# Up-projection of a fused cross-attention block: each group of 512 tokens accumulated in two halves of 256

## The chip, the cores and the metric

The kernel runs on one core of a Trainium2 chip. The metric is the device time of one execution in microseconds (us); lower is better. A measured time is the median of several executions.

## The reference

One transformer block with cross-attention, for a batch of 8, with 1024 query tokens and 64 context tokens per batch, width 512, 16 heads and a feed-forward width of 2048, all in float32:

```python
q = layer_norm(query, ln1_g, ln1_b)
qh, kh, vh = q @ wq + bq, context @ wk + bk, context @ wv + bv      # 16 heads of 32
probs = softmax(where(allowed, qh @ kh.T / sqrt(32), -inf))
x = query + (probs @ vh) @ wo + bo
h = layer_norm(x, ln2_g, ln2_b)
out = x + gelu(h @ w1 + b1) @ w2 + b2
```

The part that the change touches is `h @ w1`, the up-projection: 8192 tokens, 512 inputs, 2048 outputs.

## The kernel before

**Numbers.** A float32 product is made of three float16 products: every operand is scaled and split into a high and a low half, and `triple` accumulates high by high, high by low and low by high in PSUM, for each of the four blocks of 128 inputs. So a product over 512 inputs is 12 matmuls into one accumulation, each with a weight load of its own.

**Tiling.** The 8192 tokens are 16 chunks of 512 (`CHUNK`; `HALF` is 256). The program runs 17 slots. In slot c the attention of chunk c and the feed-forward of chunk c-1 are interleaved, so that the small dependent steps of attention are covered by feed-forward matmuls. In slot 0 there is no feed-forward, in slot 16 no attention.

**A slot on TensorE.** The loop over g has `GROUPS` = 19 turns. A turn with g below 16 makes the up-projection group g: 128 of the 2048 hidden features (the stationary operand is a 128x128 cut of `w1`) for all 512 tokens of the chunk (the moving operand is `old`, the normalised tokens with features on partitions, in the arena), into the PSUM bank `ff1_ps[:, g % 2, :]`, 128 x 512 float32. The last of the group's matmuls counts `ff1_done` up. A turn with g of 3 or more (`LAG`) makes the down-projection of group g-3 at L1384: 12 matmuls of 512 columns, whose four outputs stay in `ff2_ps` over all 16 groups. Between the two stand the attention steps that the table `PLAN` gives for that place: "Q" (48 matmuls, L1141), "S" (the scores, L1298: 24 matmuls of 128 columns; they use 64 of the 128 rows each, alternately the lower and the upper half), "V" (L1318) and "O" (L1141). All instructions of TensorE stand in one order written by the program; a slot has 624 matmuls when it has both parts.

**Who waits for a group.** ScalarE waits for `ff1_done`, reads the whole bank at L753 (gelu), then VectorE makes the two float16 halves of the result (L1114, L829). The next group but one may write the bank when the gelu is out (`g_full`); the down-projection waits for the halves (`g_lo`). In the trace `ff_ps` is both `ff1_ps` and `ff2_ps`, `at_ps` the two banks of attention, `w_all` the weights `w1` or `w2`, `act_T` and `arena` activations.

**Line L1141.** All calls of `triple` have this one line in the profile; rows are told apart by their tiles: `ff_ps<-arena,w_all` is the up-projection (3072 matmuls: 16 slots by 16 groups by 12), `at_ps<-act_T,wq` is Q and `at_ps<-wo,act_T` is O.

Of the kernel before, what the change touches and what calls it, by code (L numbers as in the profile page):

```python
# [18 lines left out]
KT = D // P  # L19
# [9 lines left out]
CHUNK = 512  # L29
TT = CHUNK // P  # L30
HALF = CHUNK // 2
# [70 lines left out]
def wait(eng, sem, value):  # L102

    if isinstance(value, int) and value <= 0:
        return
    eng.wait_ge(sem, value)


def cross_attention_block(nc, x, context, wq, wk, wv, bq, bk, bv, wo, bo,
# [5 lines left out]
    with ExitStack() as ctx:  # L115
# [144 lines left out]
        ff1_ps = ctx.enter_context(nc.psum_tensor("ff1_ps", [P, 2, CHUNK], F32))  # L260
# [109 lines left out]
        def plan(c, position):  # L370

            if isinstance(c, int) and c == 0:
                return PLAN_FIRST.get(position, [])
            second = PLAN_SECOND.get(position, []) if isinstance(c, int) and c == 1 else []
            return PLAN.get(position, []) + second
# [758 lines left out]
        def _(pe):  # L1134
            def triple(out_ap, pairs):

                last, n = None, 3 * len(pairs)
                i = 0
                for (s_hi, s_lo), (m_hi, m_lo) in pairs:
                    for s, m in ((s_hi, m_hi), (s_hi, m_lo), (s_lo, m_hi)):  # L1140
                        last = nc.tensor.matmul(out_ap, s, m, start=(i == 0), stop=(i == n - 1))  # L1141
                        i += 1
                return last
# [4 lines left out]
            for k in range(KT):  # L1148
                for n in range(KT):
                    last = nc.tensor.transpose(ff2_ps[:, k, n * P:(n + 1) * P], ctx_raw[:, n, k * P:(k + 1) * P],  # L1150
                                               ident[:, :])
# [5 lines left out]
            def maximum_rows(n):  # L1157

                if n < len(ROUNDS) - 1:
                    pe.wait_ge(max_ready[n], 1)  # L1160
                wait(pe, sums_ready, (0, 1, 3, N1 + 3, N1 + N2 + 3)[n])
                nc.tensor.transpose(turned[n], maxima[:, ROUNDS[n]], ident[:, :]).then_inc(rows_ps[n], 1)

            def maxima_everywhere(n):
                pe.wait_ge(diagonal_set[n], 1)
                nc.tensor.matmul(spread[n], ones[0:widths[n], :], on_diagonal[0:widths[n], n, 0:widths[n]],
                                 start=True, stop=True).then_inc(gmax_ps[n], 1)

            def bias_rows(n, ln_b, weight):


                quarter = P // KT
                for k in range(KT):
                    for m in range(KT):
                        w = weight(k, m)
                        last = nc.tensor.matmul(bias_bank[n][m * quarter:(m + 1) * quarter, 0:w.shape[-1]],
                                                cols[:, ln_b + k:ln_b + k + 1].to_broadcast([P, quarter]), w,
                                                start=(k == 0), stop=(k == KT - 1))
                last.then_inc(bias_rows_ps[n], 1)

            def bias_columns(n, width, rows):

                pe.wait_ge(bias_rows_set[n], 1)
                for b in range(width // P):
                    last = nc.tensor.transpose(bias_cols[n][:, b * P:(b + 1) * P], rows[:, b * P:(b + 1) * P],
                                               ident[:, :])
                last.then_inc(biases_ps[n], 1)
# [29 lines left out]
            def keys(k, m):  # L1217
                cut = slice(m * P, (m + 1) * P)
                return term(ff1_ps[:, m % 2, :], k, (wk_hi[:, k, cut], wk_lo[:, k, cut]), (ctxT_hi[:, k], ctxT_lo[:, k]))


            for k in range(KT):
                pe.wait_ge(ctx_lo, k + 1)
                pe.wait_ge(conv_lo, k + 1)
                for m in range(2):
                    last = keys(k, m)
# [5 lines left out]
            for m in range(2, KT):  # L1232
                pe.wait_ge(kv_hi, m - 1)
                for k in range(KT):
                    last = keys(k, m)
# [21 lines left out]
            def slot(c, par, attn, ff, batch):  # L1257
# [82 lines left out]
                old = hT[1 - par]  # L1340
                for g in range(GROUPS):
                    if isinstance(c, int) and c == 0 and 2 * g == BIAS_ROWS_AT:
                        for n in range(N1):
                            pe.wait_ge(w_loaded[W_1 + n], 16)
                        bias_rows(1, B2LN, lambda k, m: w1_raw[m][:, k])
                    if isinstance(c, int) and c == 0 and 2 * g == BIAS_COLUMNS_AT:
                        bias_columns(1, D, bias_rows_sb)
                    if ff and g < NJ:
                        if g % KT == 0 and isinstance(c, int) and c == 1:
                            pe.wait_ge(conv_lo, conv_w1[g // KT])  # L1350
                        if g == 0 and isinstance(c, int) and c == 1:
                            pe.wait_ge(h_lo, 4)
                        elif g == 0:
                            for n in range(TT):
                                pe.wait_ge(h_moved[n], 16 * c + (-16))
                        if g >= 2:
                            pe.wait_ge(g_full, NJ * c + (g - 1 - NJ))
                        else:
                            wait(pe, g_full, NJ * c + (-NJ))
                        cut = slice(g % KT * P, (g % KT + 1) * P)  # L1360
                        w1_hi, w1_lo = (w1_pairs[:, g // KT, a] for a in range(2))
                        triple(ff1_ps[:, g % 2, :], [((w1_hi[:, k, cut], w1_lo[:, k, cut]), (old[:, 0, k], old[:, 1, k]))
                                                     for k in range(KT)]).then_inc(ff1_done, 1)
                    if attn:
                        for kind, t in plan(c, 2 * g):
                            step(kind, t)
                    if isinstance(c, int) and c == 0:
                        for n, (rows_at, spread_at) in REDUCE_AT.items():
                            if 2 * g == rows_at:
                                maximum_rows(n)  # L1370
                            if 2 * g == spread_at:
                                maxima_everywhere(n)
                    if ff and g >= LAG:
                        j = g - LAG
                        pe.wait_ge(g_lo, NJ * c + (j + 1 - NJ))
                        if j == 0:
                            wait(pe, out_set, 4 * c + (-TT))
                        if isinstance(c, int) and c == 1:
                            pe.wait_ge(conv_lo, conv_w2[j // KT] - KT + j % KT + 1)
                        pair = g_pair[j % NG]  # L1380
                        for t in range(TT):
                            rows = slice(t * P, (t + 1) * P)
                            for i, (s, m) in enumerate(((0, w2_hi), (0, w2_lo), (1, w2_hi))):
                                last = nc.tensor.matmul(ff2_ps[:, t, :], pair[:, s, rows], m[:, j],  # L1384
                                                        start=(j == 0 and i == 0), stop=(j == NJ - 1 and i == 2))
                            if j == NJ - 1:
                                last.then_inc(ff2_done, 1)
                    if attn:
                        for kind, t in plan(c, 2 * g + 1):
                            step(kind, t)  # L1390


            for c in range(NCHUNK):
                slot(c, c % 2, True, c > 0, None if c % 2 else c // 2)
            slot(NCHUNK, 0, False, True, None)


# [18 lines left out]
```

## Time and profile before

| | us |
|---|---|
| median of 3 runs | 1868.79 |
| lowest and highest run | 1867.86, 1869.2 |
| span of the profiled execution (first to last instruction) | 1864.5 |
| TensorE busy in it | 1799.3 |
| VectorE, ScalarE, GpSimd busy in it | 1247.9, 640.5, 443.8 |

The profiled execution gives a span and no time of its own apart from it. The runs' median is 4.3 us above the span; that rest is the start and the end of the program around its instructions.

In the rows, PE is TensorE's matmuls, PEld its weight loads (which run beside matmuls), DVE is VectorE, ACT ScalarE, POOL GpSimd. Matmuls are pipelined: a matmul's recorded duration goes beyond the start of the next one, so the rate of a stream is read from starts, not from durations.

### The profile page before, as it was taken

The page shows a single profiled execution, that of the slowest core. Times are in us where ns is not written, and L with a number is a line of the kernel's source. Part 1 is how long each engine was busy: PE and PEld are TensorE (multiplying, and loading weights), DVE is VectorE, ACT ScalarE, POOL GpSimd, SP SyncE. Part 2 cuts the span into 40 slices and gives each one's busy share as a digit, 9 for nine tenths or more (in the row PEclk, how much of TensorE's full clock was granted, in tenths as well). Part 3 has the DMA queues.
Part 4 walks back from the last instruction along what each step waited for, and adds up shares of the span by engine and source line. Part 5 has one row for each costly group of instructions (what it writes and reads, how often), then busy time and mean ns, then how long its engine had stood idle before and what let it go on. Part 6 is the DMA issues. An engine that isn't in the chain of part 4 may idle for free.

```text
span 1864.5 us, 26584 instructions
## 1 busy us (share of the span) xinstructions
PE 1799.3 (97%) x10213; PEld 819.6 (44%) x10213; DVE 1247.9 (67%) x1930; ACT 640.5 (34%) x799; POOL 443.8 (24%) x376
## 2 busy tenths in 40 slices
PE   6678899999999999999999999999999999999999
PEld 3233344444444444444444444444444444444444
DVE  6767757667675767757676676757677576866622
ACT  5654424242232424223242422324242232424211
POOL 2523114131320314122141313203141221413200
PEclk8878999999999999999999999999999999999999
DMA  8230232314123241412323131332413133231200
GB/s 288 54 105 12 46 91 46 91 23 79 35 60 77 46 91 23 78 36 57 80 46 91 19 81 38 57 80 46 91 21 77 40 57 79 46 91 19 50 23 23
DMA packets 287738, 116.27 MB, mean 62 GB/s; under 512 B 262616, under 2 KB 264192, under 8 KB 287616
## 3 DMA queue, kind: packets, MB, share of 16 engines
q1 hardware_dynamic: 287616, 114.61, 27.4%
q8 instruction: 80, 1.31, 0.3%
q14 instruction: 42, 0.34, 0.1%
HBM read 31.22 MB, written 16.78 MB: 26 GB/s over the span
## 4 chain that ended last, share of the span: by engine, by line
PE 90%; DVE 5%; POOL 1%; ACT 1%; DMA 1%; issue 1%; SPq 0%; DVEq 0%; ACTq 0%
PE ff_ps L1141 34%; PE ff_ps L1384 34%; PE at_ps L1141 18%; PE at_ps L1298 2%; PE at_ps L1318 1%; DVE w_all L829 1%; POOL arena L560 1%; DVE arena L829 0%; DVE xhat L818 0%; DMA arena<-in_L_xattn_wk 0%; PE ff_ps L1213 0%; DVE arena L1114 0%; DVE arena L1061 0%; PE at_ps L1213 0%; DVE smax L1059 0%
## 5 line engine op out<-in xcount | busy, mean ns | idle before, releaser
L1141 PE MATMUL ff_ps<-arena,w_all 128*128 128x512 f16 x3072 | 701.8, 381 | 2.3 <-DVE arena L829 2.3
L1384 PE MATMUL ff_ps<-w_all,arena 128*128 128x512 f16 x3072 | 698.0, 379 | 0.9 <-DVE arena L829 0.9
L1141 PEld LDWEIGHTS ff_ps<-arena,w_all 128*128 128x128 f16 x3072 | 300.4, 98 | 371.7 <-issue 15.6
L1384 PEld LDWEIGHTS ff_ps<-w_all,arena 128*128 128x128 f16 x3072 | 294.4, 98 | 358.6 <-issue 6.4
L753 ACT ACTIVATE arena<-ff_ps,b1p,scales 128x512 f32<-128x512 f32 x256 | 198.5, 775 | 634.6 <-PE ff_ps L1141 634.3
L1114 DVE TENSOR_SCALAR arena<-arena,scales 128x512 f16<-128x512 f32 x256 | 150.1, 586 | 215.6 <-ACT arena L753 215.5
L829 DVE SCALAR_TENSOR_TENSOR arena<-arena,scales 128x512 f16<-128x512 f32 x256 | 239.2, 934 | 9.1
L511 POOL TENSOR_TENSOR rstd<-ve,minus_half 128x1 f32<-128x1 f32 x128 | 85.6, 669 | 561.1 <-DVE ve L801 561.1
L555 POOL TENSOR_TENSOR x_sb<-x_sb,bo_row 128x512 f32<-128x512 f32 x64 | 92.6, 1477 | 359.8 <-PE at_ps L1298 350.5
L687 ACT ACTIVATE norm_hl<-xhat 128x512 f16<-128x512 f32 x120 | 73.9, 628 | 287.6 <-DVE xhat L818 287.6
L560 POOL TENSOR_TENSOR arena<-arena,rsum 128x1024 f32<-128x1024 f32 x64 | 124.8, 1971 | 176.1 <-DVE rsum L1087 176.1
L1141 PE MATMUL at_ps<-act_T,wq_hi 128*128 128x512 f16 x496 | 150.0, 384 | 9.9 <-DMA act_T<-norm_hl 9.9
L1141 PE MATMUL at_ps<-wo_hi,act_T 128*128 128x512 f16 x512 | 156.9, 383 | 2.1 <-DVE act_T L829 2.1
L1044 DVE CAST qT<-arena 128x512 f16<-128x512 f32 x64 | 31.3, 489 | 125.8 <-ACT arena L691 125.8
L691 ACT ACTIVATE arena<-at_ps,bqp,scales 128x512 f32<-128x512 f32 x64 | 49.7, 778 | 159.5 <-PE at_ps L1141 155.9
L1141 PE MATMUL at_ps<-wo_lo,act_T 128*128 128x512 f16 x256 | 98.1, 383 | 0.0
L1141 PE MATMUL at_ps<-act_T,wq_lo 128*128 128x512 f16 x248 | 95.1, 384 | 0.0
L829 DVE SCALAR_TENSOR_TENSOR act_T<-at_ps,act_T 128x512 f16<-128x512 f32 x68 | 43.9, 685 | 65.3 <-ACT act_T L714 65.3
L566 POOL TENSOR_TENSOR arena<-arena,b_row 128x512 f32<-128x512 f32 x64 | 87.3, 1394 | 0.9 <-DVE xhat L818 0.9
L825 DVE TENSOR_TENSOR norm_hl<-xhat,norm_hl 128x512 f16<-128x512 f32 x120 | 83.2, 693 | 5.1 <-ACT norm_hl L687 3.6
L1059 DVE TENSOR_REDUCE smax<-at_ps 128x16 f32<-128x1024 f32 x54 | 64.9, 1202 | 26.9 <-PE at_ps L1298 26.9
L1099 DVE SCALAR_TENSOR_TENSOR arena<-at_ps,scales,x_sb 128x512 f32<-128x512 f32 x64 | 48.0, 749 | 49.6 <-PE at_ps L1141 44.4
(154 smaller groups left out, 1377.3 us busy)
## 6 DMA issues: line engine op xcount, KB each, us to landing
x_sb<-in_x SPq DMA_DIRECT2D x64, 256.0 KB, 2.8
out_x<-arena SPq DMA_DIRECT2D x64, 256.0 KB, 2.1
w_all<-in_L_xattn_w SPq DMA_DIRECT2D x6, 1024.0 KB, 11.6
arena<-in_L_xattn_w SPq DMA_DIRECT2D x2, 1024.0 KB, 15.8
v_sb<-v_sb SPq DMA_DIRECT2D x6, 192.0 KB, 3.0
arena<-in_ctx SPq DMA_DIRECT2D x1, 1024.0 KB, 5.2
arena<-in_L_xattn_wk SPq DMA_DIRECT2D x1, 1024.0 KB, 7.4
arena<-in_L_xattn_wq SPq DMA_DIRECT2D x1, 1024.0 KB, 7.4
```

The lines of the kernel that those rows point to most:

```text
L511: nc.gpsimd.tensor_tensor(rstd[:, n:n + 1], ve[:, n:n + 1], minus_half[:, :], ALU.pow).then_inc(ln_rstd, 1)
L555: nc.gpsimd.tensor_tensor(x_sb[:, t], x_sb[:, t], bo_row[:, :], ALU.add).then_inc(xb_set, 1)
L560: nc.gpsimd.tensor_tensor(pr, pr, rsum[:, t, :].unsqueeze(2).to_broadcast([P, HEADS, SC]), ALU.mult).then_inc(p_norm, 1)
L566: nc.gpsimd.tensor_tensor(x1[1 - par][:, t], x1[1 - par][:, t], b2_row[:, :], ALU.add).then_inc(x1b_set, 1)
L687: nc.scalar.activation(norm_hl[:, t, 0], xhat[:, t % 2], ACT.Copy).then_inc(n_hi, 1)
L753: nc.scalar.activation(gelu_full[g % 2], ff1_ps[:, g % 2, :], ACT.Gelu, bias=b1p[:, g:g + 1], scale=col(C1)).then_inc(g_full, 1)
L825: nc.vector.tensor_tensor(norm_hl[:, t, 1], xhat[:, t % 2], norm_hl[:, t, 0], ALU.subtract).then_inc(n_lo, 1)
L829: nc.vector.scalar_tensor_tensor(lo, src, factor, hi, ALU.mult, ALU.subtract).then_inc(done, 1)
L1059: nc.vector.tensor_reduce(smax[:, t, :], scores, AX_X, ALU.max).then_inc(s_max, 1)
L1114: nc.vector.tensor_scalar(pair[:, 0, :], gelu_full[g % 2], col(SG), None, ALU.mult).then_inc(g_hi, 1)
L1141: last = nc.tensor.matmul(out_ap, s, m, start=(i == 0), stop=(i == n - 1))
L1384: last = nc.tensor.matmul(ff2_ps[:, t, :], pair[:, s, rows], m[:, j], start=(j == 0 and i == 0), stop=(j == NJ - 1 and i == 2))
```

## The change

The 12 matmuls of an up-projection group, each of 512 tokens, become two runs of 12 matmuls of 256 tokens: the first accumulates tokens 0 to 255 into the left half of the bank, the second tokens 256 to 511 into the right half. Both use the same 12 stationary operands in the same order, and each matmul loads its own again. `ff1_done` is counted up once, by the last matmul of the second half. Nothing else is changed.

```diff
-                        triple(ff1_ps[:, g % 2, :], [((w1_hi[:, k, cut], w1_lo[:, k, cut]), (old[:, 0, k], old[:, 1, k]))
-                                                     for k in range(KT)]).then_inc(ff1_done, 1)
+                        for part in (slice(0, HALF), slice(HALF, CHUNK)):
+                            last = triple(ff1_ps[:, g % 2, part], [((w1_hi[:, k, cut], w1_lo[:, k, cut]),
+                                                                    (old[:, 0, k, part], old[:, 1, k, part]))
+                                                                   for k in range(KT)])
+                        last.then_inc(ff1_done, 1)
```

The order of instructions on TensorE in an ordinary slot, around one scores step, before (`128x512` is the shape of the moving operand; `waits` are the semaphores for which the first instruction of a row waits):

```order
L1384 MATMUL ff_ps<-w_all,arena 128x512 x11
L1141 MATMUL ff_ps<-arena,w_all 128x512 [waits g_full]
L1141 MATMUL ff_ps<-arena,w_all 128x512 x11
L1298 MATMUL at_ps<-arena,qT 128x128 [waits s_sub]
L1298 MATMUL at_ps<-arena,qT 128x128 x23
L1384 MATMUL ff_ps<-w_all,arena 128x512 [waits g_lo]
```

The same place after the change (three lines more in the file make L1384 into L1387):

```order
L1387 MATMUL ff_ps<-w_all,arena 128x512 x11
L1141 MATMUL ff_ps<-arena,w_all 128x256 [waits g_full]
L1141 MATMUL ff_ps<-arena,w_all 128x256 x23
L1298 MATMUL at_ps<-arena,qT 128x128 [waits s_sub]
L1298 MATMUL at_ps<-arena,qT 128x128 x23
L1387 MATMUL ff_ps<-w_all,arena 128x512 [waits g_lo]
```

The group has 24 matmuls of 256 columns in place of 12 of 512, and still one wait, at its first. No instruction has changed its place among the others, and the orders of the other four engines are the same.

Around the step "V" of the same slot, before:

```order
L1384 MATMUL ff_ps<-w_all,arena 128x512 x12
L1318 MATMUL at_ps<-arena 32x512 x24
L1141 MATMUL ff_ps<-arena,w_all 128x512 x12
L1318 MATMUL at_ps<-arena 32x512 x24
L1384 MATMUL ff_ps<-w_all,arena 128x512 x12
```

And after:

```order
L1387 MATMUL ff_ps<-w_all,arena 128x512 x12
L1318 MATMUL at_ps<-arena 32x512 x24
L1141 MATMUL ff_ps<-arena,w_all 128x256 x24
L1318 MATMUL at_ps<-arena 32x512 x24
L1387 MATMUL ff_ps<-w_all,arena 128x512 x12
```

Here too only the group itself differs.

## Rows read from the trace of the kernel before

**Rows 1.** The page: busy times, granted clock by slice, chain that ended last.

```profile
span 1864.5 us, 26584 instructions
...
PE 1799.3 (97%) x10213; PEld 819.6 (44%) x10213; DVE 1247.9 (67%) x1930; ACT 640.5 (34%) x799; POOL 443.8 (24%) x376
...
PEclk8878999999999999999999999999999999999999
...
PE ff_ps L1141 34%; PE ff_ps L1384 34%; PE at_ps L1141 18%; PE at_ps L1298 2%; PE at_ps L1318 1%; DVE w_all L829 1%; POOL arena L560 1%; DVE arena L829 0%; DVE xhat L818 0%; DMA arena<-in_L_xattn_wk 0%; PE ff_ps L1213 0%; DVE arena L1114 0%; DVE arena L1061 0%; PE at_ps L1213 0%; DVE smax L1059 0%
```

**Rows 2.** Busy time in stretches, PE alone: length, busy (matmuls), clock, DMA.

```profile
1000.00:1108.88 108.88, 108.88 (x626) 1.00 0.28 59
...
360.00:1700.00 1340.00, 1340.00 (x7664) 1.00 0.27 58
```

**Rows 3.** Waits of PE, 120 to 1864 us: total, times, longest.

```profile
PE at_ps L1141 <- DMA act_T<-norm_hl: 9.9, 1, 9.9
PE at_ps L1318 <- DMA arena<-qT: 5.5, 1, 5.5
PE ff_ps L1141 <- DVE arena L829: 2.3, 1, 2.3
```

**Rows 4.** The page's costliest groups: the gelu and what it waits for.

```profile
L753 ACT ACTIVATE arena<-ff_ps,b1p,scales 128x512 f32<-128x512 f32 x256 | 198.5, 775 | 634.6 <-PE ff_ps L1141 634.3
```

**Rows 5.** The chain that ended last, in order of time: start, length, matmuls.

```profile
1005.64 10.36 PE ff_ps L1384 x48
1016.00 10.36 PE ff_ps L1141 x48
```

**Rows 6.** Timeline of PE from 1060 us: start, length with the last one's tail.

```profile
1059.71 0.38 PE L1141 MATMUL ff_ps<-arena,w_all 128*128 128x512 f16 x1
1060.02 0.84 PE L1298 MATMUL at_ps<-arena,qT 64*128 64x128 f16 x24
1060.80 2.76 PE L1384 MATMUL ff_ps<-w_all,arena 128*128 128x512 f16 x12
1063.40 2.75 PE L1141 MATMUL ff_ps<-arena,w_all 128*128 128x512 f16 x12
1065.99 2.75 PE L1384 MATMUL ff_ps<-w_all,arena 128*128 128x512 f16 x12
```

**Rows 7.** Timeline of PE, first slot: two scores steps back to back.

```profile
57.01 0.84 PE L1298 MATMUL at_ps<-arena,qT 64*128 64x128 f16 x24 [2.06 <-DVE qT L1046]
57.69 1.26 PE L1298 MATMUL ff_ps<-arena,qT 64*128 64x128 f16 x24
```

**Rows 8.** Timeline of PE, first slot: part of O, below full clock.

```profile
102.15 1.06 PE L1141 MATMUL at_ps<-wo_hi,act_T 128*128 128x512 f16 x2
103.00 0.63 PE L1141 MATMUL at_ps<-wo_lo,act_T 128*128 128x512 f16 x1
103.43 1.06 PE L1141 MATMUL at_ps<-wo_hi,act_T 128*128 128x512 f16 x2
```

**Rows 9.** Short stretches of PE: length, busy (matmuls), granted clock, DMA.

```profile
101.00:105.00 4.00, 4.00 (x11) 0.50 0.54 114
...
211.00:215.00 4.00, 4.00 (x11) 0.51 0.00 0
```

**Rows 10.** Durations of single instructions at L1141 and L1298: ns min/median/max.

```profile
L1141 PEld LDWEIGHTS ff_ps<-arena,w_all x3072: 95/98/152, 120.9 to 1850.1; 128*128 128x128 f16 x192
...
L1298 PEld LDWEIGHTS at_ps<-arena,qT x1488: 92/94/148, 57.0 to 1713.9; 64*128 64x128 f16 x186
L1298 PE MATMUL at_ps<-arena,qT x1488: 215/216/312, 57.0 to 1714.0; 64*128 64x128 f16 x186
```

**Rows 11.** Timeline of PEld, the weight loads of a group in rows 6.

```profile
1063.18 2.47 PEld L1141 LDWEIGHTS ff_ps<-arena,w_all 128*128 128x128 f16 x12
```

**Rows 12.** The page: the queue that brings instructions (packets, MB, share).

```profile
q8 instruction: 80, 1.31, 0.3%
```

**Rows 13.** Timeline of PE in slot 1, behind its second wait.

```profile
210.75 4.82 PE L1141 MATMUL ff_ps<-arena,w_all 128*128 128x512 f16 x12
```

## The prediction

> **What bounds the kernel now.** I read the page first: TensorE's matmuls fill 97% of the span, no other engine passes 67%, and the chain that ended last runs through matmul lines almost alone, the up-projection with 34% of it [rows 1]. The stretches say it more sharply: between 360 and 1700 us TensorE is busy in all of the 1340 us at a granted clock of 1.00, which is the 2.4 GHz level, and one slot takes 108.88 us with not a gap in it [rows 2]. The longest waits of TensorE after 120 us are of 9.9, 5.5 and 2.3 us [rows 3], and since that stretch has no idle time, they lie before it (the program's order puts them into slot 1). The reader of the changed bank, ScalarE's gelu, spends 634 us idle waiting for the up-projection [rows 4]. So from slot 2 on a time added to a matmul stream is added to the span one for one, and everything else gains slack; the question is only what the stream of 256-column matmuls costs against that of 512.
>
> **The rate of the stream now.** In the chain, 48 matmuls of 512 columns take 10.36 us, in the down-projection and in the up-projection alike [rows 5]: 10.36 / 48 = 215.8 ns each. A change of group costs nothing on top: 1063.40 to 1065.99 is 2.59 us for 12, again 215.8 [rows 6], though the next group has another bank and other operands. At 2.4 GHz, with a column per cycle (the half-clock rows below bear that out), 512 columns last 512 / 2.4 = 213.3 ns. So 2.5 ns of each matmul are not columns, if the clock in this stretch is the full one.
>
> **Is the 2.5 ns paid by the matmul or by the column?** This decides the case: twice as many matmuls carry the same columns. Two kinds of rows answer.
> First the scores step, the shortest matmuls here (128 columns, 53.3 ns at 2.4 GHz). Its 24 go alternately to the two halves of the rows; its 24 in rows 7 take 57.69 - 57.01 = 0.68 us, far less than 24 times 53.3 ns, so two run side by side, and a pair takes 0.68 / 12 = 56.7 ns, 3.4 ns over its columns [rows 7]. The block begins with a load that nothing hides; after such a start the next group's first matmul takes about 0.01 us more (2.76 against 2.75 [rows 6]), and without it the pair is at 55.8 ns, 2.5 over its columns. Reading steps of 0.01 us are worth 0.8 ns here, so the cost at 128 columns is 1.7 to 3.4 ns.
> Second, at half clock: three matmuls of O take 103.43 - 102.15 = 1.28 us [rows 8] where the granted clock is 0.50, the 1.2 GHz level [rows 9]. That is 426.7 ns each, exactly 512 / 1.2, and 1.977 times 215.8, not twice. A cost in proportion to columns would double with the clock; this one is there at full clock and gone at half.
> So the extra is a fixed 2.5 ns per matmul at full clock, and a matmul of 256 columns takes 106.7 + 2.5 = 109.2 ns.
>
> **Are the doubled weight loads hidden?** There are 3072 more. A load of 128 columns is recorded at 98 ns [rows 10]. The loads of the group that starts at 1063.40 begin at 1063.18 [rows 11], one matmul ahead: each load lies under the matmul before its own. At 109.2 ns there is room for 98, with 11 to spare; and the scores show that less room is enough, since loads recorded at 94 ns are followed by matmuls every 56.7 ns on the same half of the rows [rows 7, 10]. I cost them at nothing. Where that cover fails, it can be read too: the scores' rows differ from the group's before them, the load comes only behind it, and the first scores matmul starts 0.31 us after the last of the group (1059.71 to 1060.02 [rows 6]) and not 0.216: 0.09 us for one uncovered load.
> The Trainium skill, page "TensorE: Matmul & The Clock Gate", section "Back-to-back issue gap", speaks against the change: with a weight load per matmul it gives a sustained 81 ns at 128 columns, well over the columns' time. Section "LDWEIGHTS (loading the stationary operand)" of the same page gives a load as columns divided by 1.2, an estimate of 107 ns here, which would leave 2 ns of room. This trace has 56.7 ns where the page has 81, and 98 where it has 107; by the page's 25 ns over, paid by each new matmul, the estimate would be some 140 us more, by the rows nothing.
>
> **The other parts.** (a) Instructions: the queue that brings them moved 1.31 MB in 80 packets [rows 12] for 20,426 matmuls and loads [rows 1], about 64 bytes each; 6,144 more are 0.39 MB or 24 packets. It is at 0.3% of the DMA engines, and TensorE has taken 24 loads and 24 matmuls in 0.68 us [rows 7] where a changed group has 2.6 us for as many. Nothing. (b) The count of `ff1_done` and the wait for `g_full` stay one per group, at its end and its start. The gelu cannot start on the first half, so there is no gain from it; it starts as much later as the group has become longer, and its engine waits anyway [rows 4]. (c) The bank: before, 12 matmuls added to the same 512 columns one after the other; now to the same 256. The scores do the same on 128 at the fixed cost above. Nothing.
>
> **The sum.** A group has 12 matmuls more: 12 x 2.5 = 30 ns. Of 256 groups, 9 do not count. Four stand in slot 1 before its 9.9 us wait and four between the last scores step and the 5.5 us wait [rows 3], both for transposes that do not depend on them. One, at 210.75, runs at the half-clock level [rows 9, 13], where there is no fixed cost. So 247 x 12 = 2964 added matmuls x 2.5 ns = 7.4 us. The span becomes 1864.5 + 7.4 = 1871.9; the runs' median stands 4.3 us above the span (1868.79 - 1864.5), which I leave as it is: **1876.2 us**, 0.4% slower.
> Its bounds: 2.5 ns is sure at 512 columns; at 128 it is 1.7 to 3.4. At 256, a third of the way from 128 to 512, that leaves 2.0 to 3.1. A pair of halves then costs twice that less 2.5, 1.4 to 3.7 ns more than the whole, and 2964 times that is 4.3 to 11.0 us: 1873.1 to 1879.8.
>
> **Rivals.**
> A. The cost goes by the column (the clock is really a little under 2.4 GHz where 1.00 is shown), and two halves are as long as the whole. Then nothing changes: 1868.8 us, not slower. For it: a clock of 1.00 has two digits, and 2.5 ns is 1.2%. Against it: a scores pair would take 128 x 215.8 / 512 = 54.0 ns, 0.65 us for rows 7's 0.68; and the half-clock rows show no such part. It decides below 1.9 ns per matmul at 256 columns (2 x 1.9 - 2.5 = 1.3 ns, 3.7 us in all, 0.2% of the time, which is about what a measurement here tells from no change). 7%.
> B. Loads show. In its small form, at the seam, the first load of the second half is not taken ahead and costs 0.09 us in 247 groups, 22 us: 1898 us. In its large form each short matmul pays for its load what a scores pair pays over its columns when the uncovered start is spread on it: 1060.80 - 1060.02 = 0.78 us for 12 pairs is 65 ns, 11.7 over 53.3 [rows 6], so 2 x 118.4 - 215.8 = 21 ns for 2964, 62 us: 1938 us. For it: the room of 11 ns is thin beside 98. Against it: no group change shows a seam, and full rows should not need more than two half-row loads in 56.7 ns. It decides where load and hand-over together pass 109 ns. The page's 81 ns is a rule of this kind. 5%.
>
> **How the numbers follow.** The forecast has 87%, A 7%, B 5%; 1% is left for a gain that I have no mechanism for. Faster by over 0.2%: 1%. Within 0.2%: A and the lowest edge of the forecast, 8%. Slower: 91%. The range is the forecast's own, 1873 to 1880 us; A and B together may stay outside.
>
> **What would show it.** In the profile after: 6144 up-projection matmuls of 256 columns, 96 of them in 10.48 us where 48 took 10.36; a group 2.62 us in place of 2.59; a slot 109.36 in place of 108.88; loads still at 98 ns, one matmul ahead; no new wait of TensorE between 360 and 1700 us; the down-projection still at 2.59. If 96 take 10.36, A holds; if the first matmul of the second half comes 0.2 us after the one before it, B's seam; if all stand 118 ns apart, B's large form. I would be wrong in another way if the longer program itself let TensorE wait for its instructions, as gaps without a releaser.

## The result and the profile after

The changed kernel takes 1875.77 us (median of 4 runs, 1874.94 to 1877.4); the kernel before, beside it, 1868.73. The ratio is 1.0041, with a 95% interval of 1.0027 to 1.0056: about 7.0 us slower. The forecast was 1876.2 us, and slower.

From the page of the changed kernel, the lines that answer to [rows 1], [rows 4] and [rows 12], and the costliest matmul and load groups:

```profile
span 1873.1 us, 32728 instructions
...
PE 1806.7 (96%) x13285; PEld 1121.4 (60%) x13285; DVE 1247.9 (67%) x1930; ACT 640.6 (34%) x799; POOL 444.1 (24%) x376
...
PEclk8878999999999999999999999999999999999999
...
q8 instruction: 104, 1.70, 0.4%
...
L1141 PE MATMUL ff_ps<-arena,w_all 128*128 128x256 f16 x6144 | 709.5, 274 | 2.3 <-DVE arena L829 2.3
L1387 PE MATMUL ff_ps<-w_all,arena 128*128 128x512 f16 x3072 | 698.0, 379 | 1.6 <-DVE arena L829 1.6
L1141 PEld LDWEIGHTS ff_ps<-arena,w_all 128*128 128x128 f16 x6144 | 602.2, 98 | 121.7 <-issue 9.3
L753 ACT ACTIVATE arena<-ff_ps,b1p,scales 128x512 f32<-128x512 f32 x256 | 198.6, 776 | 640.0 <-PE ff_ps L1141 639.6
```

TensorE has 3072 matmuls and 3072 loads more. The loads are recorded at the same 98 ns. VectorE, ScalarE and GpSimd are as busy as before to 0.3 us; ScalarE's idle time behind the up-projection has grown from 634.3 to 639.6 us, so it takes the longer groups as slack. The instruction queue moved 0.39 MB in 24 packets more, as forecast.

The rate itself, from the chain of the changed kernel that ended last (start, length, matmuls), which answers to [rows 5]:

```profile
1775.98 10.36 PE ff_ps L1387 x48
1786.34 10.48 PE ff_ps L1141 x96
```

10.48 / 96 = 109.2 ns for a matmul of 256 columns, against 10.36 / 48 = 215.8 for one of 512, in the same execution. Two halves take 218.3, 2.5 ns more than the whole. The timeline of the changed kernel's TensorE (start, length with the last one's tail) shows where in a group it lies:

```profile
1002.42 2.78 PE L1141 MATMUL ff_ps<-arena,w_all 128*128 128x256 f16 x24
1005.04 2.75 PE L1387 MATMUL ff_ps<-w_all,arena 128*128 128x512 f16 x12
1007.63 2.78 PE L1141 MATMUL ff_ps<-arena,w_all 128*128 128x256 f16 x24
```

A group begins 2.62 us before what follows it, where [rows 6] had 2.59; the down-projection is still at 2.59. From one step V to the same step of the next slot the traces have 108.89 us before and 109.37 after. A stretch of the changed kernel, cut at the forecast 109.36 us, shows TensorE busy in all of it (length, busy, clock, DMA; above it the long stretch), to be held against [rows 2]:

```profile
360.00:1700.00 1340.00, 1340.00 (x9969) 1.00 0.28 59
1000.00:1109.36 109.36, 109.36 (x817) 1.00 0.27 59
```

No wait was added in it. The waits of the changed kernel's TensorE after 120 us (total, times, longest) are those of [rows 3]; the last has grown by 0.7 us:

```profile
PE at_ps L1141 <- DMA act_T<-norm_hl: 9.8, 1, 9.8
PE at_ps L1318 <- DMA arena<-qT: 5.4, 1, 5.4
PE ff_ps L1141 <- DVE arena L829: 2.3, 1, 2.3
PE ff_ps L1387 <- DVE arena L829: 1.6, 1, 1.6
```

The two profiled spans differ by 8.6 us, more than the medians. The end of the last wait shows why. First the kernel before, then the changed one, from the timelines of their TensorE:

```profile
251.03 2.76 PE L1384 MATMUL ff_ps<-w_all,arena 128*128 128x512 f16 x12 [0.92 <-DVE arena L829]
```

```profile
252.44 2.76 PE L1387 MATMUL ff_ps<-w_all,arena 128*128 128x512 f16 x12 [1.61 <-DVE arena L829]
```

From here to the end it is 1864.5 - 251.03 = 1613.47 us before and 1873.1 - 252.44 = 1620.66 after: 7.19 us more, for the 240 groups of slots 2 to 16, 30 ns each. The other 1.4 us lie ahead of it, in the start and in slot 1, where this point also moves between kernels whose groups are alike (252.44 to 254.01 us in the runs below with 24 matmuls a group). The tables below therefore give the time from this point to the end too, as "tail". It scatters far less: the change, inter and uneven, whose groups are as long as each other, have tails within 0.1 us.

### The profile page after: what moved, and what is told of

Same layout as the page of the kernel before. It is cut to its first block, busy times and chain, and to the rows that moved or that the text cites. A ratio compares the mean times of both kernels' runs of the same rounds, so it can differ in the third digit from the quotient of the medians.

```text
span 1873.1 us, 32728 instructions
## 1 busy us (share of the span) xinstructions
PE 1806.7 (96%) x13285; PEld 1121.4 (60%) x13285; DVE 1247.9 (67%) x1930; ACT 640.6 (34%) x799; POOL 444.1 (24%) x376
## 4 chain that ended last, share of the span: by engine, by line
PE 90%; DVE 5%; POOL 1%; ACT 1%; DMA 1%; issue 1%; SPq 0%; DVEq 0%; ACTq 0%
PE ff_ps L1141 34%; PE ff_ps L1387 34%; PE at_ps L1141 17%; PE at_ps L1298 2%; PE at_ps L1318 1%; DVE w_all L829 1%; POOL arena L560 1%; DVE arena L829 0%; DVE xhat L818 0%; DMA arena<-in_L_xattn_wk 0%; PE ff_ps L1213 0%; DVE arena L1114 0%; DVE arena L1061 0%; PE at_ps L1213 0%; DVE smax L1059 0%
## 5 line engine op out<-in xcount | busy, mean ns | idle before, releaser
L1141 PE MATMUL ff_ps<-arena,w_all 128*128 128x256 f16 x6144 | 709.5, 274 | 2.3 <-DVE arena L829 2.3
L1387 PE MATMUL ff_ps<-w_all,arena 128*128 128x512 f16 x3072 | 698.0, 379 | 1.6 <-DVE arena L829 1.6
L1141 PEld LDWEIGHTS ff_ps<-arena,w_all 128*128 128x128 f16 x6144 | 602.2, 98 | 121.7 <-issue 9.3
L1387 PEld LDWEIGHTS ff_ps<-w_all,arena 128*128 128x128 f16 x3072 | 294.4, 98 | 330.9 <-issue 6.4
L753 ACT ACTIVATE arena<-ff_ps,b1p,scales 128x512 f32<-128x512 f32 x256 | 198.6, 776 | 640.0 <-PE ff_ps L1141 639.6
L1141 PE MATMUL at_ps<-act_T,wq_hi 128*128 128x512 f16 x496 | 150.1, 385 | 9.8 <-DMA act_T<-norm_hl 9.8
L1141 PE MATMUL at_ps<-wo_hi,act_T 128*128 128x512 f16 x512 | 157.0, 383 | 2.1 <-DVE act_T L829 2.1
L1141 PE MATMUL at_ps<-wo_lo,act_T 128*128 128x512 f16 x256 | 98.1, 383 | 0.0
L1141 PE MATMUL at_ps<-act_T,wq_lo 128*128 128x512 f16 x248 | 95.2, 384 | 0.0
L1141 PEld LDWEIGHTS at_ps<-act_T,wq_hi 128*128 128x128 f16 x496 | 48.9, 99 | 69.8 <-issue 12.9
L1141 PEld LDWEIGHTS at_ps<-wo_hi,act_T 128*128 128x128 f16 x512 | 50.5, 99 | 64.9 <-issue 5.7
```

The lines of the kernel that those rows point to most:

```text
L753: nc.scalar.activation(gelu_full[g % 2], ff1_ps[:, g % 2, :], ACT.Gelu, bias=b1p[:, g:g + 1], scale=col(C1)).then_inc(g_full, 1)
```

## The experiments

The theory: at full clock each matmul has a fixed 2.5 ns that its columns do not explain, and the doubled loads are hidden. The rivals: the cost comes with the weight loads; it comes at the start of the second accumulation or at the change between halves; loads would show soon. Every edit is to the up-projection group unless said otherwise. "Tail more" is against the 1613.47 us of the kernel before, and each time stands beside the kernel before on the same chip.

| run | us | before, us | ratio, 95% interval | tail more, us |
|---|---|---|---|---|
| change | 1875.77 | 1868.73 | 1.0041, 1.0027 to 1.0056 | 7.19 |
| quarters | 1892.09 | 1867.32 | 1.0133, 1.0118 to 1.0149 | 21.61 |
| extra_loads | 1868.24 | 1867.32 | 1.0004, 0.9995 to 1.0013 | 0.59 |
| inter | 1875.42 | 1867.32 | 1.0042, 1.0029 to 1.0056 | 7.28 |
| uneven | 1876.35 | 1867.32 | 1.0044, 1.0030 to 1.0058 | 7.22 |
| both | 1882.31 | 1868.11 | 1.0080, 1.0065 to 1.0096 | 14.40 |
| eighths | 1919.23 | 1868.11 | 1.0276, 1.0261 to 1.0292 | 50.80 |
| uneven32 | 1901.25 | 1868.11 | 1.0180, 1.0166 to 1.0194 | 33.02 |
| halves_extra_loads | 1876.79 | 1867.45 | 1.0048, 1.0034 to 1.0062 | 7.99 |
| uneven_extra_loads | 1950.67 | 1867.45 | 1.0445, 1.0429 to 1.0461 | none: no wait at this point |

**quarters: four accumulations of 128 tokens.**

```diff
-                        for part in (slice(0, HALF), slice(HALF, CHUNK)):
+                        for part in (slice(n * P, (n + 1) * P) for n in range(KT)):
```

> Each group as four accumulations of 128 tokens, 48 matmuls in place of 12. Fixed cost per matmul (2.5 ns at full clock, loads hidden): 36 x 2.5 = 90 ns for each of 247 groups, 22.2 us over the kernel before, 1890.9 us; a matmul every 55.8 ns, the group 2.68 us. Cost by the column: 1868.7. Loads that must have ended (98 ns as recorded) before their matmul starts: a matmul every 98 ns at least, 2.1 us per group, some 2390 us. The page's sustained 81 ns would be 1.3 us per group, some 2190 us (an estimate).

Measured 24.8 us over the kernel before, its interval 22.0 to 27.8; the tail has 21.61, and 240 groups at 90 ns are 21.6. The chain of this run:

```profile
1790.19 10.36 PE ff_ps L1387 x48
1800.56 10.72 PE ff_ps L1141 x192
```

10.72 / 192 = 55.8 ns: 53.3 of columns and 2.5. It is the same fixed part at 128 columns, now on all 128 rows and with a full load for each; no spacing of 98 ns shows. Nor does the sustained 81 ns that the Trainium skill gives for 128 columns (page "TensorE: Matmul & The Clock Gate", section "Back-to-back issue gap"): the measurement decides, 55.8 ns.

**extra_loads: the kernel before, each load made twice.** As many loads as in the change, as many matmuls as before.

```diff
+                                nc.tensor.ldweights(s[:, k, cut])
                                 last = nc.tensor.matmul(ff1_ps[:, g % 2, :], s[:, k, cut], old[:, m, k],
```

> The kernel before, with 12 matmuls of 512 tokens per group, and every weight load of the up-projection made twice: as many loads as in the halved kernel, as many matmuls as before. Fixed cost per matmul: two loads (2 x 98 ns) hide under one matmul (215.8), 1868.7 us. Cost that comes with each load: 2.5 ns x 2964 more loads, 1876.1 us. If only one load can stand ready and the second waits until the first is used up: up to 98 ns for each of 3072, 2170 us.

The page of this run shows that the loads were made, its chain that they cost nothing in the stream:

```profile
PE 1801.4 (97%) x10213; PEld 941.3 (50%) x13285; DVE 1248.4 (67%) x1930; ACT 640.6 (34%) x799; POOL 443.9 (24%) x376
```

```profile
1769.92 10.36 PE ff_ps L1388 x48
1780.28 10.36 PE ff_ps L1365 x48
```

10.36 for 48, as before. The interval holds no change and excludes 7 us. So the 2.5 ns does not come with a load; it comes with a matmul. One thing stays untested: every matmul of every run has a load of its own, so a price for taking over the loaded operand, paid once per matmul, cannot be told from a price of the matmul itself.

The 0.59 us in the tail can be placed. They lie behind the step V that stands before an up-projection group, where no matmul hides the group's first loads. First the kernel before, then this run, from the timelines of their TensorE:

```profile
1084.21 0.84 PE L1318 MATMUL at_ps<-arena 64*32 64x512 f16 x24
1084.98 2.76 PE L1141 MATMUL ff_ps<-arena,w_all 128*128 128x512 f16 x12
```

```profile
1086.00 0.84 PE L1318 MATMUL at_ps<-arena 64*32 64x512 f16 x24
1086.82 2.77 PE L1365 MATMUL ff_ps<-arena,w_all 128*128 128x512 f16 x12
```

From V's start to the group's it is 0.77 us before and, read in ns, 0.81 here: 0.039 us more in each of 14 slots, 0.55 us. So an extra load that no matmul covers does cost, some 40 ns.

**inter: both halves in turn for each stationary operand, one accumulation start for the bank.**

```diff
+                        for k in range(KT):
+                            for i, (s, m) in enumerate(((w1_hi, 0), (w1_hi, 1), (w1_lo, 0))):
+                                for part in (slice(0, HALF), slice(HALF, CHUNK)):
+                                    last = nc.tensor.matmul(ff1_ps[:, g % 2, part], s[:, k, cut], old[:, m, k, part],
+                                                            start=(k == 0 and i == 0 and part.start == 0),
...
```

> The same 24 matmuls of 256 tokens per group as in the change, in another order: for each of the 12 stationary operands both halves in turn, as one accumulation over the bank, so that the second half never starts an accumulation of its own and each stationary operand is loaded twice in a row. Fixed cost per matmul: as the change, 1875.8 to 1876.2 us. A cost of 30 ns at the start of the second accumulation: 1868.7. A cost for changing between halves: 23 changes per group in place of 1, far above 1876.

This run is as long as the change, in time and in tail, and its up-projection too takes 10.48 us for 96. So neither a second accumulation nor the changes between halves cost anything that shows; the number of matmuls counts.

**uneven: 448 and 64 tokens.**

```diff
-                        for part in (slice(0, HALF), slice(HALF, CHUNK)):
+                        for part in (slice(0, 7 * SC), slice(7 * SC, CHUNK)):
```

> Halves of unequal size, 448 and 64 tokens: 24 matmuls per group and the same columns. Fixed cost per matmul with loads hidden even under 64 columns (26.7 + 2.5 = 29.2 ns): as the change, 1876 us. If a load of all rows needs 56 ns of its own (what a pair of half-row loads is seen to fit into in the scores): 27 ns for 12 x 247 matmuls, 80 us, 1956. If it needs the 98 ns recorded: 69 ns each, 204 us, 2080. A granted clock that falls in the groups would add to any of these.

The time is that of the change again. TensorE's timeline of this run (a row is named by its first matmul's shape):

```profile
1009.20 2.78 PE L1141 MATMUL ff_ps<-arena,w_all 128*128 128x448 f16 x24
1011.82 3.40 PE L1387 MATMUL ff_ps<-w_all,arena 128*128 128x512 f16 x15
```

The group takes 1011.82 - 1009.20 = 2.62 us, as in the change, though half of its matmuls offer a load only some 29 ns of cover.

**both: the down-projection in halves too.** Each of its matmuls becomes two of 256 columns, in turn, as in inter.

```diff
-                                last = nc.tensor.matmul(ff2_ps[:, t, :], pair[:, s, rows], m[:, j],
+                                for part in (slice(0, HALF), slice(HALF, CHUNK)):
+                                    last = nc.tensor.matmul(ff2_ps[:, t, part], pair[:, s, rows], m[:, j, part],
...
```

> The change, and the down-projection's matmuls too in halves of 256 columns (each stationary operand used for both halves in turn). Fixed cost per matmul: 3072 more matmuls in a second place, of which 240 to 250 groups count, 7.2 to 7.5 us over the change, 14.6 over the kernel before, 1882 us. A cost that belongs to the up-projection or its bank alone: 1876. The next group's first load starts up to 0.1 us later, which should hide.

The tail grows by 14.40 us, which is 480 groups at 30 ns. The chain of this run:

```profile
1783.19 10.48 PE ff_ps L1388 x96
1793.67 10.48 PE ff_ps L1141 x96
```

The price is the same in another loop, with other operands and another bank, and adds up.

**eighths: eight accumulations of 64 tokens**, by the same edit with parts of 64.

> Each group as eight accumulations of 64 tokens, 96 matmuls, a whole group at 29.2 ns each. Fixed cost per matmul: 84 x 2.5 = 210 ns for 247 groups, 51.9 us over the kernel before, 1919 us, the group 2.80 us. If the loads hide only in short bursts of such matmuls (12 in the run with 448 and 64) and not in 96: more, up to 98 ns each, 9.4 us per group. If the granted clock falls to its lower level in them, the group takes up to twice as long and the 512-column matmuls behind it too.

```profile
1817.82 10.36 PE ff_ps L1387 x48
1828.18 11.20 PE ff_ps L1141 x384
```

In its chain 11.20 / 384 = 29.2 ns, 26.7 and 2.5; 240 x 210 ns is 50.4 of the 50.80 us in the tail. The granted clock stays at 1.00 between 360 and 1700 us, without a gap.

**uneven32: 480 and 32 tokens**, by the edit of uneven with 32.

> Unequal halves of 480 and 32 tokens: 24 matmuls per group, the same columns. Fixed cost per matmul with hidden loads (32 columns: 13.3 + 2.5 = 15.8 ns): 1876 us, as the change. If a full load and its hand-over need up to the 29.2 ns that the 64-column matmuls of the run with 448 and 64 took (the shortest seen so far): up to 13.4 ns for each of 2964, 40 us more, 1916.

Here the fixed price ends. The chain of this run:

```profile
1800.72 10.37 PE ff_ps L1387 x48
1811.09 10.91 PE ff_ps L1141 x96
```

A pair takes 10.91 / 48 = 227.3 ns; with 202.5 for 480 columns (200.0 and 2.5, and so the starts in the trace stand), 24.8 are left for 32 columns, where 13.3 + 2.5 would be 15.8. Both numbers of the expectation missed; 9.0 ns for 2880 matmuls are 25.9 us of its tail.

**halves_extra_loads and uneven_extra_loads: each load twice, in the change and in uneven**, by the edit of extra_loads.

> The change, with every weight load of the up-projection made twice: two loads to each matmul of 256 columns (109.2 ns). If a load takes 98 ns of the array's time as recorded, two do not fit: 196 in place of 109.2, 87 ns for each of 6144 matmuls, some 530 us more than the change. If a load takes no more than the 29.2 ns that a load and a 64-column matmul were seen to need, two hide with room to spare: 1876 us, as the change.

> Halves of 448 and 64 tokens, with every weight load made twice: two loads to each matmul of 29.2 ns. If the 24.8 ns at which the 32-column matmuls stood is the time of a load, two take 49.6 ns, 20.4 more for 12 matmuls of 247 groups, 60 us: 1936. If the 24.8 ns is a floor of the matmul itself and a load takes less than 14.6 ns, nothing changes: 1876. In the run of 512 columns with doubled loads the second load was recorded 41 ns after the first; if that is the time of a load, two take 82 ns, 53 more for each of 2964, 157 us: 2033.

Two loads hide under one matmul of 256 columns: the chain has 10.48 us for 96 (last line of the first fence), and the time is that of the change. Its tail has 0.80 us more than the change, 0.55 us of it again behind the step V. Under 64 columns two loads show. The second fence is TensorE's timeline of uneven_extra_loads, the third its matmuls of 64 columns from the third to the twelfth (the last of its first row stands again as its second row):

```profile
1777.83 10.36 PE ff_ps L1389 x48
1788.19 10.48 PE ff_ps L1366 x96
```

```profile
1007.25 3.10 PE L1366 MATMUL ff_ps<-arena,w_all 128*128 128x448 f16 x24
1010.18 2.75 PE L1389 MATMUL ff_ps<-w_all,arena 128*128 128x512 f16 x12
```

```profile
1009.62 0.72 PE L1366 MATMUL ff_ps<-arena,w_all 128*128 128x64 f16 x10
1010.14 0.20 PE L1366 MATMUL ff_ps<-arena,w_all 128*128 128x64 f16 x1
```

That group takes 2.93 us in place of 2.62, 26 ns more for each of the 12 short matmuls on average. Inside, they stand (1010.14 - 1009.62) / 9 = 58 ns apart, where with one load they stood 29.2. All three values of the expectation missed, the nearest being 49.6. So a load in such a stream takes some 29 ns or less, not the 98 recorded. Whether the 24.8 ns of uneven32 is a load or a floor of the matmul stays open: one load fits into 24.8 ns there, but two take 58 and not 49.6 here.

**Not tried:** a gelu that starts when the first half is done. Both halves lie in one PSUM bank, and nothing in the program would then order ScalarE's reading of it against TensorE's writing of the second half.

## Why the prediction was right

**What bounds it.** That a time added to the stream is added to the span held from slot 2 on: 240 groups at 30 ns, and 7.19 us in the tail.

**2.5 ns per matmul, not per column.** This was the step that decided. Chains give it at 512 and 256 columns (215.8 and 109.2), at 128 (55.8) and at 64 (29.2), on all rows; extra_loads takes the load out of the question, inter the seam. The scores block from which the prediction read its 128 columns was indeed at full clock, which the prediction did not show (length, busy, clock of the kernel before):

```profile
57.01:57.69 0.68, 0.68 (x25) 1.00 0.00 0
```

In ns, the pairs of that block stand 56 apart but for the first step, which is 66 to 67: the 0.01 us that the prediction took off for the start was right. The half-clock step has its counterpart in slot 1 of the changed kernel, in the group that answers to [rows 13]. The first line is the stretch (length, busy, clock), the other two are TensorE's timeline; the last matmul of the row of 16 is the first of the row behind it:

```profile
211.60:215.40 3.80, 3.80 (x19) 0.50 0.00 0
```

```profile
211.80 3.62 PE L1141 MATMUL ff_ps<-arena,w_all 128*128 128x256 f16 x16
215.00 0.63 PE L1141 MATMUL ff_ps<-arena,w_all 128*128 128x256 f16 x2
```

(215.00 - 211.80) / 15 = 213.3 ns for a matmul of 256 columns at the lower level, 256 / 1.2 exactly and half of the 426.7 of [rows 8]: no price there. (The clock rises within this group, in both kernels: its last matmuls stand 110 ns apart here. So the group as a whole is no test.) What the 2.5 ns is made of no run shows.

**Loads at nothing.** Right, with far more room than the 11 ns that were read off the record: extra_loads and halves_extra_loads hide twice as many where a matmul covers them. The recorded 98 ns is how long a load lasts, not how often one can be made; the loads of the scores, 94 ns long every 56.7 on the same rows, had said so.

**The sum.** 7.4 us forecast, about 7.0 measured by the medians, with an interval of 5.0 to 10.5. One small step was read wrongly: the 4.3 us between median and span were called the start and the end of the program. The changed kernel's profiled run has a time of its own, 1874.94 us, only 1.8 over its span; most of the 4.3 was the difference of one execution from another. It did not enter the difference of the kernels. Of the 247 groups the tail shows 240; the seven of slot 1 cannot be read, since that slot scatters by more than their 0.2 us.

**The rivals.** A (by the column) fell with 10.48 against 10.36. From 64 to 512 columns a matmul grows by (215.8 - 29.2) / 448 = 0.4165 ns a column, 2.40 columns a ns, so the clock is not below 2.4 GHz. B's seam (1898) and its large form (1938) fell with the even 109.2 ns; loads show only where two are made for 64 columns, or where nothing covers the second, as behind step V. The 1938 was also added up wrongly: the 62 us hold the 2.5 ns already, so it should have been 1868.8 + 62 = 1931. The "some 140 us" is loose too: 25 ns for each of 2 x 2964 matmuls is 148. Neither entered the forecast.

No run was faster than the kernel before: its feed-forward matmuls already have 512 columns, the whole width of the bank `ff1_ps[:, g % 2, :]`, and no run tried wider ones.

## What to carry to other kernels

Where TensorE has no gaps, count matmuls as well as columns: at full clock each cost 2.5 ns here beyond its columns, down to 64 columns, so halving a stream's width cost 1.2% of that stream (2.5 of 215.8 ns) and cutting it into eighths 8% (0.21 of 2.59 us). Read the price of a short matmul from the shortest stream in the same trace and from the same stream at the other clock before you blame weight loads. To see whether loads are hidden, double them: here that told more than their recorded duration.

## What was not expected of the hardware

Full weight loads, recorded at 98 ns, hid under matmuls of 64 columns 29.2 ns apart, 96 in a row. With two for each, such matmuls stood 58 ns apart. Matmuls of 32 columns stood 24.8 ns apart and not 15.8. At the lower clock, matmuls of 256 columns stood 213.3 ns apart, with nothing beyond their columns.
